# A one-core transformer kernel: rounded rows of its last stage turned by a DMA, with other orders of steps

## What is computed

```python
x = x + _L1_attn_ref(_layernorm(x, axis=-1), L1_attn_weight_qkv, L1_attn_weight_proj)
x = x + _L1_xattn_ref(_layernorm(x, axis=-1), ctx_2048)
x = x + _L1_ffn_ref(_layernorm(x, axis=-1), L1_ffn_w1, L1_ffn_w2, L1_ffn_w3)
```

```python
def quant_dequant_act_1x128(x):
    xb = x.reshape(E, M, K // BLK, BLK)
    amax = jnp.max(jnp.abs(xb), axis=-1, keepdims=True)
    safe = jnp.maximum(amax, ACT_EPS)
    q = (xb * (FP8_MAX / safe)).astype(jnp.float8_e4m3fn)
    return (q.astype(jnp.float32) * (safe / FP8_MAX)).reshape(E, M, K)
...
    return jnp.einsum('emk,enk->emn', xq, wq)
```

## Time and profile before

| | |
|---|---|
| median of three runs | 1042.27 us |
| the profiled execution | 1039.38 us |
| its span, first to last instruction | 1037.3 us |
| granted TensorE clock, mean | 0.998 |
| TensorE matmuls busy | 1003.9 us, 97% |
| VectorE busy | 836.0 us, 81% |
| ScalarE busy | 661.0 us, 64% |
| GpSimd busy | 442.0 us, 43% |

### The profile page before, as it was taken

The page is one execution under the profiler, slowest core; times in us unless marked ns, Lnnn a source line. Parts: engine busy times, 40 slices in busy tenths (PEclk is TensorE's granted clock), DMA queues, the critical chain, the costliest instruction groups (busy, mean ns, idle before and its releaser), DMA issues.

```text
span 1037.3 us, 15005 instructions
## 1 busy us (share of the span) xinstructions
PE 1003.9 (97%) x4949; PEld 742.1 (72%) x4949; DVE 836.0 (81%) x1751; ACT 661.0 (64%) x1252; POOL 442.0 (43%) x655
## 2 busy tenths in 40 slices
PE   7999999999999999999999999998999999999998
PEld 6787788778887887665766888876766666666544
DVE  6898878787787787658899688786989979979975
ACT  5755555555555554356556576854579889898774
POOL 3435224422432233337887432024645635635420
PEclk9999999999999999999999999999999999999999
DMA  8443333333333432272100164310001112112223
GB/s 300 180 153 106 98 113 102 102 93 112 102 102 103 113 92 82 94 306 98 41 1 1 32 243 145 130 41 1 1 11 34 35 35 49 35 40 44 35 59 79
DMA packets 100860, 91.90 MB, mean 89 GB/s; under 512 B 79152, under 2 KB 80432, under 8 KB 96432
## 3 DMA queue, kind: packets, MB, share of 16 engines
q1 hardware_dynamic: 100784, 90.96, 28.4%
HBM read 56.69 MB, written 15.60 MB: 70 GB/s over the span
## 4 chain that ended last, share of the span: by engine, by line
PE 68%; DVE 16%; ACT 7%; issue 5%; POOL 4%; DVEq 0%; ACTq 0%; POOLq 0%
PE bank L471 51%; PE bank L555 4%; PE bank L943 3%; PE bank L479 3%; PE bank L546 1%; PE bank L566 1%; PE bank L485 1%; DVE ctx_lo L1308 1%; DVE wgt L1066 1%; DVE eu L1269 1%; DVE at L1571 1%; DVE prod L1559 1%; ACT squares L2223 1%; DVE fm L1701 1%; DVE x L1615 1%
## 5 line engine op out<-in xcount | busy, mean ns | idle before, releaser
L471 PE MATMUL bank<-win_hi,a_uT_hi 128*128 128x512 f32 (+1 forms) x320 | 125.4, 392 | 3.5 <-DVE win_lo L1023 2.6
L471 PE MATMUL bank<-win_lo,a_uT_hi 128*128 128x512 f32 (+1 forms) x320 | 119.8, 374 | 0.0
L471 PE MATMUL bank<-win_hi,a_uT_lo 128*128 128x512 f32 (+1 forms) x320 | 119.3, 373 | 0.0
L2421 POOL TENSOR_TENSOR y<-y,off 128x512 f32<-128x512 f32 x24 | 37.9, 1580 | 91.5 <-DVE off L1085 91.5
L471 PEld LDWEIGHTS bank<-win_hi,a_uT_hi 128*128 128x128 f32 x320 | 60.2, 188 | 17.4 <-DVE win_lo L1023 4.2
L1066 DVE TENSOR_SCALAR wgt<-cum_all,neg 128x128 f32<-128x128 f32 x256 | 67.9, 328 | 0.4 <-DMA cum_all<-cum_rows 0.4
L471 PEld LDWEIGHTS bank<-win_hi,a_uT_lo 128*128 128x128 f32 x320 | 60.2, 188 | 11.2
L1800 ACT ACTIVATE zs<-y 128x1024 uint16<-128x1024 uint16 x30 | 31.7, 1057 | 56.6 <-DVE y L1100 56.6
L471 PEld LDWEIGHTS bank<-win_lo,a_uT_hi 128*128 128x128 f32 x320 | 60.3, 188 | 9.3 <-issue 0.2
L471 PE MATMUL bank<-f,fqT_next 128*128 128x512 fp8e4 (+1 forms) x312 | 64.0, 362 | 0.0
L555 PEld LDWEIGHTS bank<-xs,wgt 128*128 128x128 f32 x512 | 59.9, 192 | 2.4 <-issue 1.0
(11 more groups left out here) (348 smaller groups left out, 3011.7 us busy)
## 6 DMA issues: line engine op xcount, KB each, us to landing
cum_all<-cum_rows SPq DMA_DIRECT2D x16, 1024.0 KB, 4.8
wchunk<-w_in SPq DMA_DIRECT2D x32, 256.0 KB, 5.6
y_rows<-zs SPq DMA_DIRECT2D x30, 256.0 KB, 2.0
stage<-f_in SPq DMA_DIRECT2D x3, 1408.0 KB, 6.1
x<-x_in SPq DMA_DIRECT2D x16, 256.0 KB, 5.6
land<-win_in SPq DMA_DIRECT2D x4, 1024.0 KB, 8.3
wq<-ctxT_in SPq DMA_DIRECT2D x4, 1024.0 KB, 6.5
out<-x SPq DMA_DIRECT2D x16, 256.0 KB, 2.0
```

What stands on the lines that cost most here:

```text
L471: made = e.matmul(bank, a, b, start=start and n == 0, stop=stop and n == len(pairs) - 1)
L2421: e.tensor_tensor(y[m % 2][:, cols], y[m % 2][:, cols], off[:], ALU.add).then_inc(sig("y_off"), 1)
```

## The change

The rounded tile is no longer multiplied back before it is turned. to_fp8's last operation writes the rounded values to a bf16 tile eq, and one DMA transpose turns it to eqT. The 4 factors of each of the 128 rows (am row 2) go to DRAM in the order block, row, 4 bytes at a time, and come back as one row of 512 numbers broadcast to 128 partitions, into eT. GpSimd multiplies eT by eqT in place. The second scale_eu, turn_eu and keep_eT are gone. The ring of fqT has 4 buffers instead of 6. All five loops have another order; n runs to NT + 18; the lag of the store on SP is 16. The filler of turn_eu stands in e_product.

```diff
@@ tensor_program
-            def turn_eu(n):
-                bank = banks.claim(w, ("eu", n), "eT_ready", n + 1)
-                if n in (0, 1, NT - 3):
-                    keep_busy(bank, 6)
-                w.wait_ge("eu_ready", n + 1)
-                turn(bank, eu[n % 2], KD, ident).then_inc(sig("eu_turned"), 1)
             def e_product(n):
...
+                if n in (0, 1, NT - 3):
+                    keep_busy(bank, 6)
                 w.wait_ge("eT_ready", n + 1)
@@ the loop of tensor_program, after the change
                if t3 is not None:
                    qkv_product(t3, 1)
                if t6 is not None:
                    e_product(t6)
                if t4 is not None:
                    turn_o(t4)
                if t7 == NT - 1:
                    turn_last_fq()
                if t2 is not None:
                    turn_du(t2)
                if t10 is not None:
                    f_down(t10)
                if t4 is not None:
                    attend_out(t4)
                if t7 is not None:
                    f_up(t7)
...
                        scatter(k)
                if t2 is not None:
                    qkv_product(t2, 0)
@@ vector_program
-                e.tensor_tensor(val, val, tmp, ALU.subtract).then_inc(sig(done), 1)
+                if n and rounded is not None:
+                    w.wait_ge("eq_turned", 16 * n)
+                e.tensor_tensor(val if rounded is None else rounded, val, tmp, ALU.subtract).then_inc(sig(done), 1)
...
-                to_fp8(eu[n % 2][:], et[:], "e_fp8", n)
+                to_fp8(eu[n % 2][:], et[:], "e_fp8", n, eq[:])
@@ scalar_program
-            def keep_eT(n):
-                w.wait_ge("eu_turned", n + 1)
-                w.wait_ge("crossed", n)
-                e.activation(eT[:], banks.of["eu", n][:], ACT.Copy).then_inc(sig("eT_ready"), 1)
...
-                if t11 is not None:
-                    scale_eu(t11, 2, "e_back", "eu_ready")
@@ gpsimd_program
+            def scale_turned(n):
+                w.wait_ge("es_spread", 16 * (n + 1))
+                w.wait_ge("eq_turned", 16 * (n + 1))
+                e.tensor_tensor(eT[:], eT[:], eqT[:], ALU.mult).then_inc(sig("eT_ready"), 1)
@@ sync_program
+            def put_scales(n):
+                w.wait_ge("e_back", n + 1)
+                e.dma_start(es_rows.ap()[n].rearrange("(k t) -> t k", k=KD), am[:, 2, :], allow_slow_non_contiguous=True).then_inc(
+                    sig("es_out"), 16)
+
+            def spread_scales(n):
+                w.wait_ge("es_out", 16 * (n + 1))
+                if n:
+                    w.wait_ge("crossed", n)
+                e.dma_start(eT[:], es_rows.ap()[n:n + 1, :].broadcast_to(
+                    [P, P * KD])).then_inc(sig("es_spread"), 16)
+
+            def turn_eq(n):
+                w.wait_ge("e_fp8", n + 1)
+                if n:
+                    w.wait_ge("eT_ready", n)
+                e.dma_start_transpose(turned_by_tiles(eqT[:]), eq[:]).then_inc(sig("eq_turned"), 16)
...
                 if t6 is not None and t6 < NT - 1:
                     turn_fq(t6)
-                if t9 is not None:
-                    store(t9)
+                if t4 is not None:
+                    put_scales(t4)
+                    turn_eq(t4)
+                    spread_scales(t4)
                 if t7 is not None and t7 < NT - 1:
                     turn_hq(t7)
+                if t16 is not None:
+                    store(t16)
```

More of the change, by code:

```diff
@@ L414, in decoder_kernel @@
         fq = spread("fq", 1, [P, D], BF16, parts=late)[0]
-        fqT = spread("fqT", 1, [P, D], BF16, parts=after_ternary) + spread("fqT_next", 5, [P, D], BF16, parts=late + work)
+        fqT = spread("fqT", 1, [P, D], BF16, parts=after_ternary) + spread("fqT_next", 3, [P, D], BF16, parts=late + work)
+        eq, eqT = spread("eq", 2, [P, D], BF16, parts=late + work)
         hq = spread("hq", 1, [P, HID], BF16)[0]
@@ L946, in tensor_program @@
             banks.use(sorted(range(8), key=lambda k: banks.banks[k] in accs))
-            for n in range(NT + 15):
-                t0, t1, t2, t3, t4, t5, t6, t7, t8, t9, t10, t11, t12, t13, t14, t15 = behind(n, 16)
+            for n in range(NT + 18):
+                t0, t1, t2, t3, t4, t5, t6, t7, t8, t9, t10, t11, t12, t13, t14, t15, t16, t17, t18 = behind(n, 19)
+                if t3 is not None:
+                    qkv_product(t3, 1)
                 if t6 is not None:
@@ L954, in tensor_program @@
                     turn_last_fq()
+                if t2 is not None:
+                    turn_du(t2)
                 if t10 is not None:
                     f_down(t10)
-                if n < len(scattered_by) - 1:
-                    for k in range(scattered_by[n], scattered_by[n + 1]):
-                        scatter(k)
                 if t4 is not None:
@@ L963, in tensor_program @@
                     f_up(t7)
+                if n < len(scattered_by) - 1:
+                    for k in range(scattered_by[n], scattered_by[n + 1]):
+                        scatter(k)
                 if t2 is not None:
                     qkv_product(t2, 0)
[L966 to L973, removed]
         def vector_program(e):
@@ L1258, in vector_program, with to_fp8 @@
             dotted = []
-            def to_fp8(val, tmp, done, n):
+            def to_fp8(val, tmp, done, n, rounded=None):
                 if n:
@@ L1714, in vector_program @@
             w.wait_ge("q_step", 8 * BATCH)
-            for n in range(NT + 15):
-                t0, t1, t2, t3, t4, t5, t6, t7, t8, t9, t10, t11, t12, t13, t14, t15 = behind(n, 16)
+            for n in range(NT + 18):
+                t0, t1, t2, t3, t4, t5, t6, t7, t8, t9, t10, t11, t12, t13, t14, t15, t16, t17, t18 = behind(n, 19)
+                if t3 is not None:
+                    attend_weights(t3)
+                if n == 1:
+                    low_du(0)
+                if t10 is not None:
+                    add_down(t10)
+                if t6 is not None:
+                    f_scale(t6)
                 if n == 0:
@@ L2295, in scalar_program @@
             w.wait_ge("q_step", 8 * BATCH)
[L2296 to L2299, removed]
-                if t11 is not None:
-                    e_centre(t11)
-                if t13 is not None:
-                    f_quantise(t13)
+            for n in range(NT + 18):
+                t0, t1, t2, t3, t4, t5, t6, t7, t8, t9, t10, t11, t12, t13, t14, t15, t16, t17, t18 = behind(n, 19)
                 if t9 is not None:
                     keep_qkv(t9, 0)
+                if t7 is not None:
+                    square(t7, 0)
+                if t9 is not None:
                     keep_qkv(t9, 1)
-                if n == 3:
-                    high_proj()
                 if t14 is not None:
@@ L2336, in scalar_program @@
                     d_normal(t7)
-                if t11 is not None:
-                    keep_eT(t11)
+                if t10 is not None:
+                    e_centre(t10)
+                if t12 is not None:
+                    f_round(t12)
+                if t10 is not None:
+                    square(t10, 1)
+                if t12 is not None:
+                    f_quantise(t12)
         def gpsimd_program(e):
@@ L2734, in gpsimd_program @@
                     low_proj()
+                if t11 is not None:
+                    scale_turned(t11)
                 if t10 is not None:
```

122 lines of the change are left out of this document (56 added, 66 removed).

## The result

The changed kernel takes 1121.7 us (median of 4, 1111.6 to 1124.1), the kernel before 1043.2 beside it (4 runs): a ratio of 1.0745, 95% interval 1.0706 to 1.0784. It is **slower by 7.5%, 78 us**, where the forecast was 4 us faster.

The account below looks back on a forecast made before the run. TensorE, at 97% of the span, was taken to bound the kernel. Stage terms summed to -4.3 us: 1035.1 for the profiled execution, 1038.0 us against the median of 1042.27, range 1031 to 1044.5.

Parts of the forecast that it names:

- the put's: SP writes the scales to DRAM in 4-byte pieces: landing 1.3 to 4.8 us, costed at nothing, up to 2 us behind early rounding.
- no term below is a matter of the clock: Throughout the last stage the granted clock was 1.00, the full 2.4 GHz, so no forecast term depended on it.
- fill to the first product: Start of the last stage: longer path against an earlier attend_out, 0, give or take 1.5 us.
- second step: Tile with four keys: 18.0 us from product to product where it took 17.0, so +1.0 us.
- three steps from there: Steps from 751 us, 18.95 each: 17.6 in the first two, 18.2 in the third, so -3.2 us.
- eight middle steps: 808 to 960 us, 19.03 on average: TensorE needs 18.4, 0.5 left in each of two long-tile passes; -3.9 us.
- next two steps: 960 to 994 us: last long tile's loop and tile 14's path take about what they replace, 0.
- to the last product: Longer path in the drain: last product at 1007.7 against 1006.22, so +1.5 us; saved turn and copy swallowed.
- behind it (stores): Stores slip seven steps but drain by 1034, before the last is issued: +0.3 us, up to 3.
- Late scales: Spread lands later than 3.2 us: gain gone at 3.9, 5 us slower at 4.8, +13 at 5.5; chance 0.16.
- VectorE held: Each GpSimd multiply holds one VectorE operation by 0.78 us; gain only -1 us, within 0.5%; chance 0.12.
- The path is not what counts: The reordering alone could pay or cost; no size and no chance of its own.

Follow-up runs that it names:

- the kernel with 16-byte pieces: Changed kernel, with the four scales of a token written to DRAM as one 16-byte piece; 1036.2 us, 0.9950 of the kernel before.
- the kernel with the new way alone: Step order of the kernel before, but e scaled through DRAM (16-byte put, spread, DMA turn, GpSimd multiply); 1082.6 us, 1.0393 of the kernel before.

## Why the prediction was wrong

**The step that failed** is the put's: "It is issued once e_back is done, six us before the rounding in a full step, so I cost it at nothing", with bounds of 1.3 and 4.8 us. Its landing is 8.2 us (7.7 to 10.6 in the kernel with GpSimd's queue in another order), and 8.51 in the changed kernel's own chain above. My rows for the bounds were DMAs with long rows on both sides; cum_rows moves 8 KB, four times as much, in 1.3 us, but in 512-byte pieces. The one thing that set this DMA apart, 4-byte pieces interleaved in DRAM, stood in the diff and in my own sentence, and I priced it by its bytes. With a landing under the upper bound the step holds: 1.4 and 3.1 us both cost nothing that shows.

**A second omission made it large.** I followed the path from rounding to product and asked what covers it, and never from the put back to itself. The put, spread, multiply, the deviation behind the multiply in GpSimd's queue, e_scales, e_back and the next put are a loop; I wrote that GpSimd "is no bound" from its busy time (12.58 of 19.55 us), which is true and says nothing of an instruction that waits at the head of its queue. Cutting the loop in that queue recovered 61 us with the slow put in place.

**A third**: "no term below is a matter of the clock". That held for the kernel before and nearly holds for each fast version (0.993 to 0.997 in the whole span); once long waits came in, the clock added about 27 us.

**The rest, against the kernel with 16-byte pieces,** whose landing is what I had assumed (span 1035.3 against 1037.3):

| stage | forecast | measured |
|---|---|---|
| fill to the first product | 0 | +1.3 |
| second step | +1.0 | +0.5 |
| three steps from there | -3.2 | -4.5 |
| eight middle steps | -3.9 | -3.9 |
| next two steps | 0 | +0.7 |
| to the last product | +1.5 | +2.1 |
| behind it (stores) | +0.3 | +1.9 |
| sum | -4.3 | -2.0 |

By the prediction's own figures the three steps give about -3.4, not -3.2. The +1.9 behind the last product's start is not the stores but the clock: TensorE has waited 3.2 us there, and its eight matmuls take 5.49 us in the kernel with 16-byte pieces where the earlier trace rows have 3.67 for such a product; the windows give the granted clock from 1002.36 to 1008.00 us as 0.70.

```profile
1002.36 5.49 PE L474 MATMUL bank<-wq,eT 128*128 128x512 f32 x8 [3.22 <-POOL eT L2660]
```

What follows it, stores included, takes as long as before within 0.1 us.

By the medians it is 3.4 us faster, by the ratio 0.5% (forecast 4.3 and 0.4%). Middle steps of 18.48 us against "18.4 to 18.5", the spread's landing of 3.6 us against 3.2, the multiply of 1.43 us in this form (1.15 in the changed kernel's) against 1.27, and ScalarE at 15.0 us a step against "under 15.5" stand as forecast. So the mechanism of the gain was right; it was the put that swallowed it twenty times over.

**The rivals.** *Late scales* had the right kind of event, scales landing late, and the wrong cause (the spread, not the put) and size: +13 us at the most, since it priced delays in single steps and no loop. *VectorE held* had its event right and its price wrong. In the kernel with 16-byte pieces 10 of the 20 adds of attend_add (L1597) overlap the new multiply and take over 0.9 us where an undisturbed one takes 0.68; the mean of all 20 goes from 805 to 1150 ns. VectorE in the timeline, with the multiply between:

```profile
875.81 0.68 DVE L1597 TENSOR_TENSOR o<-o,pv 128x512 f32<-128x512 f32 x1
876.61 1.42 POOL L2660 TENSOR_TENSOR eT<-eT,eq 128x512 f32<-128x512 f32 x1 [0.71 <-DMA eT<-es_rows]
876.88 1.69 DVE L1597 TENSOR_TENSOR o<-o,pv 128x512 f32<-128x512 f32 x1
```

It is not paid, for two reasons. VectorE is not full in such a step (17.92 of 18.48 us), and the rounding got shorter: the two-input add of the rounding that took 1.470 us at its median in the earlier trace rows takes 0.693 (691 to 707 ns over its 16 instances), now that it runs at another time of the step (in the old order with the new way it is back at 1.48, as that kernel's chain shows). VectorE's busy time in the whole kernel is 830.9 us against 836.0. A hold stands inside the loop of the changed kernel, too: VectorE's smallest operation of e_scales (L1627, 128x4) takes 1.148 us at its median there (0.94 in the chain above), beside GpSimd's next attention product, and 0.229 in the kernel with 16-byte pieces, so 0.7 to 0.9 of the 21.15 us are a hold. Whether GpSimd causes these holds was not tried by itself. *The path is not what counts* was held "inside the first three"; alone, order and new way are worth 0 and +41 us, together -5 (1.0003, 1.0393 and 0.9950). They can only be priced as a pair.

## What to carry to other kernels

Price a DMA by what its smallest pieces touch, not by its bytes: where a transposing view makes different partitions write neighbouring 4-byte words of DRAM, turn the view round, even if a reader must then stride. When a change adds a round trip through DRAM, follow it from its own issue back to its next issue through every queue in which something stands behind it; that length is a floor for the step, and it can be cut by the order of one queue. When such a floor makes TensorE wait, reckon the clock as a second price.

## What was not expected of the hardware

- 128 pieces of 4 bytes that touch land in 6.9 us, the same 128 pieces 2048 bytes apart in 1.4, and 512 of them 64 bytes apart in 2.4.
- The spread of 256 KB landed in 5.0 us (median) in the changed kernel, where it is issued as soon as the put has landed, and in 3.6 to 3.7 in the kernels where the put had landed a while before. Behind the quick 16-byte put, issued as soon as that has landed, it took 3.9. Why was not tried.
- Twelve useless matmuls ahead of every crossing product's wait took about 27 us off a kernel of 1122.
- Weights read 16 bytes apart cost TensorE next to nothing: the 8 matmuls of an e product take 3.79 us in the chain of waits of the kernel with the new way alone, against 3.67 in the earlier trace rows. The multiply on such a view takes 1.43 us for 1.15 (medians; 1.64 in the kernel with the spread ahead of the turn).
- A wait of 3.2 us ahead of one product went with a granted clock of 0.70 behind it, and with 5.49 us for work of 3.67.
